# VectorE's attention and evictions in another order, projections one product earlier, the last operands h in the token buffers, stores behind the loads

## The reference

```python
xn = layernorm(x)
# attention: 32 heads of 16, 8 key/value heads, each token for itself
q, k, v = xn @ Wq + bq, xn @ Wk + bk, xn @ Wv + bv
k, v = repeat(k, 4), repeat(v, 4)
scores = einsum('bsdh,bseh->bsde', q, k) / 4        # 16 x 16 per token
s = einsum('bsde,bseh->bsdh', softmax(scores), v)
# gated feed-forward, 1792 hidden
nx = xn * rsqrt(mean(xn**2) + 1e-5) * ln_w
y = (silu(nx @ gate_w.T) * (nx @ up_w.T)) @ down_w.T
out = x + s * silu(y)
```

## Time and profile before

| | |
|---|---|
| three runs | 504.86 us median, 503.04 to 504.94 |
| profiled execution | 505.15 us, of which the span is 503.0 us |
| PE busy | 479.9 us (95%), 2148 matmuls |
| PEld busy | 394.8 us (78%) |
| DVE busy | 404.1 us (80%) |
| ACT busy | 225.1 us (45%) |
| POOL busy | 104.1 us (21%) |
| granted TensorE clock, mean | 0.996 |
| transfers | 105.12 MB, 209 GB/s |

### The profile page before, as it was taken

One profiled execution on the slowest core, in us unless ns is written; L12 is line 12 of the kernel. 1 busy time (PEld: TensorE's weight loads), 2 busy tenths in 40 slices (PEclk: granted clock), 3 DMA queues, 4 the chain that ended last, 5 costly groups with the idle time before them and its releaser, 6 DMA issues.

```text
span 503.0 us, 6150 instructions
## 1 busy us (share of the span) xinstructions
PE 479.9 (95%) x2148; PEld 394.8 (78%) x2148; DVE 404.1 (80%) x552; ACT 225.1 (45%) x373; POOL 104.1 (21%) x85
## 2 busy tenths in 40 slices
PE   7989999999999999989799989999999999999995
PEld 6778888777778888768788777887878788888873
DVE  6889788889889797849995968878886886876784
ACT  4573555576576564572113142432244243245222
POOL 3703222222222362335222101111111111112000
PEclk9999999999999999999899999999999999999999
DMA  8803799666666755772253557755555555414582
GB/s 256 319 1 151 289 331 362 247 249 250 249 247 246 264 219 213 251 270 95 85 170 123 182 215 248 294 189 208 208 210 210 188 188 189 188 43 153 185 289 85
DMA packets 27310, 105.12 MB, mean 209 GB/s; under 512 B 2832, under 2 KB 4112, under 8 KB 23952
## 3 DMA queue, kind: packets, MB, share of 16 engines
q1 hardware_dynamic: 27280, 104.74, 57.2%
HBM read 68.29 MB, written 36.44 MB: 208 GB/s over the span
## 4 chain that ended last, share of the span: by engine, by line
PE 57%; DVE 23%; ACT 8%; issue 7%; DMA 3%; SPq 1%; POOL 1%; DVEq 0%; ACTq 0%
PE gu_ps L430 12%; PE gu_ps L433 11%; PE gu_ps L432 11%; PE y_ps L561 4%; PE y_ps L560 4%; PE y_ps L562 4%; DVE prod L1063 3%; DVE scores L1066 2%; PE gu_ps L560 2%; PE gu_ps L562 2%; PE gu_ps L561 2%; DVE z_lo L980 2%; DVE prod L1081 2%; DMA xz<-x 2%; DVE attn L1084 1%
## 5 line engine op out<-in xcount | busy, mean ns | idle before, releaser
L430 PE MATMUL gu_ps<-z_hi,w_ops 128*128 128x512 f32 x364 | 143.8, 395 | 3.9 <-DVE h_kept L1044 1.5
L432 PE MATMUL gu_ps<-z_lo,w_ops 128*128 128x512 f32 x364 | 141.8, 390 | 0.0
L433 PE MATMUL gu_ps<-z_hi,w_ops 128*128 128x512 f32 x364 | 141.8, 390 | 0.0
L430 PEld LDWEIGHTS gu_ps<-z_hi,w_ops 128*128 128x128 f32 x364 | 68.3, 188 | 25.4 <-issue 6.5
L387 POOL TENSOR_TENSOR h_lo<-h,h_hi 128x512 fp32r<-128x512 f32 x28 | 38.3, 1370 | 204.3 <-ACT h_hi L792 204.3
L433 PEld LDWEIGHTS gu_ps<-z_hi,w_ops 128*128 128x128 f32 x364 | 68.3, 188 | 14.5
L432 PEld LDWEIGHTS gu_ps<-z_lo,w_ops 128*128 128x128 f32 x364 | 68.3, 188 | 13.4
L560 PE MATMUL y_ps<-wd_ops,h_hi 128*128 128x512 f32 x168 | 66.2, 394 | 2.4 <-POOL h_lo L387 2.3
L561 PE MATMUL y_ps<-wd_ops,h_hi 128*128 128x512 f32 x168 | 65.8, 391 | 0.0
L562 PE MATMUL y_ps<-wd_ops,h_lo 128*128 128x512 f32 x168 | 65.8, 391 | 0.0
L792 ACT ACTIVATE h_hi<-h 128x512 fp32r<-128x512 f32 x28 | 17.7, 632 | 98.3 <-DVE h L1032 98.3
(11 more groups left out here) (108 smaller groups left out, 747.6 us busy)
## 6 DMA issues: line engine op xcount, KB each, us to landing
w_kept<-w_ops SPq DMA_DIRECT2D x13, 1792.0 KB, 5.7
w_ops<-w_kept SPq DMA_DIRECT2D x13, 1792.0 KB, 7.4
wd_ops<-wd_kept SPq DMA_DIRECT2D x42, 512.0 KB, 4.0
raw<-gate_up SPq DMA_DIRECT2D x28, 256.0 KB, 3.3
wd_kept<-wd_ops SPq DMA_DIRECT2D x14, 512.0 KB, 7.2
xz<-x SPq DMA_DIRECT2D x16, 256.0 KB, 5.6
raw<-down SPq DMA_DIRECT2D x14, 256.0 KB, 7.3
xz<-x SPq DMA_DIRECT2D x2, 1024.0 KB, 5.8
```

The source lines that it names most:

```text
L430: pe.matmul(acc, w_h, z_hi[:, zi, c, :], start=start and c == 0, stop=False, skip_group_check=True)
L432: pe.matmul(acc, w_h, z_lo[:, zi, c, :], start=False, stop=False, skip_group_check=True)
L433: end = pe.matmul(acc, w_l, z_hi[:, zi, c, :], start=False, stop=c == 1, skip_group_check=True)
```

## The change

1. **Tokens' buffers for h.** From `FREE` = 43 on, `h_place(u)` puts both parts of h in `z_hi` and `z_lo`, which nobody reads after the last `m3`. Each of these 13 items has a place of its own, so ScalarE no longer waits for a buffer, but for the last `m3`. GpSimd makes all remainders, VectorE's `h_lo_part` is gone.
2. **Shares.** Each group has three portions: between `c12` and `times_up1` (second pass only), ahead of `c22`, behind it. The second pass has 104 steps in groups 14 to 27 instead of 114, the burst 29 instead of 35, so 33 steps instead of 17 are left behind the last group. `finish(1, j)` stands in groups 17, 18, 20 and 21 instead of 17 to 20.
3. **Takes earlier.** In the burst a take stands behind each portion and the `t_lo` behind the take, so product 8 is taken before any `t_lo`.
4. **Projections.** Product 3 runs before the first `gate1`; the second pass's eight each run one item earlier. On ScalarE `z_hi_tile` of tiles 5 to 7 and item 17's h stand earlier among `z_raw_tile`.
5. **Start.** The sum of the q bias goes from VectorE (one reduce) to GpSimd (two adds, between two `scale_tile`), and `lo_a(1)` goes ahead of take 4, take 6 ahead of `lo_s(1)`.
6. **Stores.** `store(2)` goes behind the last load.
7. ScalarE's last exponential comes behind all h; `t_hi(1, 3)` goes ahead of `y_out(1, ...)`.

```diff
+        FREE = ITEMS - NI + 1
+        def h_place(u):
+            if u < FREE:
+                return h_hi[:, u % 2, :], h_lo[:, u % 2, :]
+            m, c = divmod(u - FREE, 2)
+            return z_hi[:, m, c, :], z_lo[:, m, c, :]
...
-        PAIR_SHARES = (((0, 0), (1, 1), (2, 2), (2, 2), (2, 2), (2, 2), (2, 2), (2, 2), (0, 1), (1, 1), (1, 2),
-                        (2, 2), (1, 2), (1, 2)), ((5, 5),) + ((5, 3),) * (NI - 1))
-        SUM_SHARE = 2
-        BURST_SHARES = (5, 4, 4, 4, 3, 3, 3, 3)
+                       ((0, 3, 4), (0, 3, 2), (1, 5, 2), (1, 4, 2), (1, 4, 2), (1, 5, 2), (1, 4, 2), (1, 4, 2))
+                       + ((1, 5, 2),) * (NI - 8))
+        FINISH_IN = (3, 4, 6, 7)
+        BURST_SHARES = (2, 2, 2, 3, 4, 4, 5, 4, 3)
...
             def h_lo_part(u):
                 blk, n = item(u)
+                hi, lo = h_place(u)
                 pool.wait_ge(h_hi_done, u + 1)
-                wait(pool, d_done, J * (u - 1))
+                if u < FREE:
+                    wait(pool, d_done, J * (u - 1))
...
             scale_tile(J)
+            pool.wait_ge(bias_in, 48)
+            bias_quads = bq_raw.rearrange("p (n s r) -> p n s r", s=2, r=2)
+            pool.tensor_tensor(bias_quads[:, :, :, 0], bias_quads[:, :, :, 0], bias_quads[:, :, :, 1], ALU.add)\
+                .then_inc(bias_summed, 1)
+            pool.wait_ge(bias_summed, 1)
+            pool.tensor_tensor(bias[:, 0:DG], bias_quads[:, :, 0, 0], bias_quads[:, :, 1, 0], ALU.add)\
+                .then_inc(bias_summed, 1)
             scale_tile(J + 1)
...
             second_tile(J + 3)
+            qkv_product(3)
             gate1(0)
...
             for u in range(NI + 2, 2 * NI - 1):
                 down_product(u)
-                if u >= NI + 3 and u - NI - 3 < JJ:
-                    qkv_product(JJ + u - NI - 3)
+                if u - NI - 2 < JJ:
+                    qkv_product(JJ + u - NI - 2)
...
-                wait(act, d_done, J * (u - 1))
+                if u < FREE:
+                    wait(act, d_done, J * (u - 1))
+                else:
+                    act.wait_ge(m3_done, GROUPS)
...
             for u in range(ITEMS - NI, ITEMS):
                 load_wd(u)
-                if u == ITEMS - 4:
-                    store(2)
+            store(2)
             store(3)
```

More of the change, by code:

```diff
@@ L418, in _ @@
                     rms_of(0, JJ, 3, JJ)
-            for u in range(NI, LO_LAST):
+            for u in range(NI, ITEMS):
                 h_lo_part(u)
@@ L558, in down_tile @@
                 acc = gu_ps[:, j, :] if u >= 2 * NI and blk else y_ps[:, j, :]
[L559 to L563, removed]
+                hi, lo = (part[:, j * P:(j + 1) * P] for part in h_place(u))
+                pe.matmul(acc, hi, wd_ops[:, u % 3, 0, :], start=n == 0, stop=False)
+                pe.matmul(acc, hi, wd_ops[:, u % 3, 1, :], start=False, stop=False)
+                pe.matmul(acc, lo, wd_ops[:, u % 3, 0, :], start=False, stop=n == NI - 1).then_inc(d_done, 1)
             def down_product(u):
@@ L613, in _ @@
             second_tile(J + 3)
+            qkv_product(3)
             gate1(0)
             up1(0)
-            for index in range(3, JJ - 1):
+            for index in range(4, JJ - 1):
                 qkv_product(index)
@@ L871, in _ @@
             h_hi_part(NI + 2)
+            z_hi_tile(1, 5)
             z_raw_tile(1, 4)
-            for j in range(5, JJ):
-                z_hi_tile(1, j)
-                z_raw_tile(1, j)
+            z_hi_tile(1, 6)
+            z_raw_tile(1, 5)
             h_hi_part(NI + 3)
+            z_raw_tile(1, 6)
+            z_hi_tile(1, 7)
+            z_raw_tile(1, 7)
             for u in range(NI + 4, 2 * NI):
@@ L890, in _ @@
                 if g == NI + 1:
+                    t_hi(1, 3)
                     for j in range(J):
@@ L1166, in _ @@
             qkv_take(5)
+            qkv_take(6)
             lo_s(1)
[L1168 removed]
             t_lo(0, 3)
@@ L1172, in _ @@
                     c12(g - 1)
+                attention(shares[g][0])
                 if g + 1 < NI:
@@ L1196, in _ @@
                     lo_s(g + 1)
-                attention(shares[g][1])
+                attention(shares[g][2])
                 times_up0(g)
@@ L1205, in _ @@
                 t_add(1, n)
-            for n in range(3):
-                t_lo(1, n)
-                attention(SUM_SHARE)
-            for index in range(JJ, 2 * JJ):
-                qkv_take(index)
-                attention(BURST_SHARES[index - JJ])
+            for n, steps in enumerate(BURST_SHARES):
+                attention(steps)
+                if n < JJ:
+                    qkv_take(JJ + n)
+                if n < 3:
+                    t_lo(1, n)
             for j in range(J):
                 finish(0, j)
-            attention(shares[NI][0])
+            attention(shares[NI][1])
             times_up0(NI)
-            attention(shares[NI][1])
+            attention(shares[NI][2])
             times_up1(NI)
+            t_lo(1, 3)
             for g in range(NI + 1, GROUPS):
@@ L1221, in _ @@
                     c12(g - 1)
+                    attention(shares[g][0])
                     times_up1(g - 1)
-                else:
-                    t_lo(1, 3)
-                if 3 <= g - NI < 3 + J:
-                    finish(1, g - NI - 3)
-                attention(shares[g][0])
+                if g - NI in FINISH_IN:
+                    finish(1, FINISH_IN.index(g - NI))
+                attention(shares[g][1])
                 c22(g)
-                attention(shares[g][1])
+                attention(shares[g][2])
                 times_up0(g)
@@ L1232, in _ @@
             times_up1(LAST)
-            for u in range(LO_LAST, LO_LAST + 3):
-                h_lo_part(u)
-                attention(2)
+            attention(6)
             assert taken[0] >= values_end(3 * J - 1)
-            for u in range(LO_LAST + 3, ITEMS):
-                h_lo_part(u)
-                if u - LO_LAST - 3 < J:
-                    finish(2, u - LO_LAST - 3)
-                else:
-                    attention(3)
+            for j in range(J):
+                finish(2, j)
+                attention(4)
             attention(STEPS)
```

63 lines of the change are left out of this document (23 added, 40 removed).

## The result

The changed kernel takes 501.36 us (median of seven runs, 499.45 to 502.16) against 504.86 for the kernel before (seven runs, 503.04 to 505.81): ratio 0.9929, 95% interval 0.9909 to 0.9948. Forecast were 500.5 and a range of 493 to 506. The profiled execution, the slowest of the seven, took 502.16 us, span 500.4.

What follows compares the result with a forecast made beforehand. TensorE, busy 95% of the 503.0 us span, was taken as the bound. From 505.15: start +1.2, middle -8.8, groups -1.8, end +4.8 give 500.55, stated as 500.5; range 493.0 to 506.

Steps and rivals of the forecast that it cites:

- Start, +1.2 forecast: Up to m1(1): take 4 behind lo_a(1) comes at 42.3, product 6 waits 2.6 us; +1.2 us.
- the bound of +3.2: Start's upper bound: take 0 is 0.9 late and the clock falls as it did at 244 us.
- 0.5 later: Start: take 0 between 0.5 earlier and 0.8 later with GpSimd's bias adds; 0.5 later taken.
- Middle, -8.8 forecast: Where the second pass begins: waits for h_lo, take 8 and times_up(14) go, no clock fall; -8.8 us.
- The 0.4 that I charged: Middle: t_hi(1, 3) and four y_out fall ahead of take_u2(15) with no stall to cover them; 0.4 us lost.
- Rival B: Middle: GpSimd remainders keep takes late, second stall and clock fall stay (4.4 us); 504.9, no change; chance 0.15.
- Groups, -1.8 forecast: Groups 15 to 27: three waits for a seed and small gaps come to 2.2 us, 0.4 left; -1.8 us.
- End, +4.8 forecast: After group 27: 33 steps and GpSimd's remainders delay VectorE's last chain from 495.05 to 499.8; +4.8 us.
- GpSimd's share was 7.8 forecast: End: of 13 remainders costing 15 us, the part falling on VectorE moves its last chain from 492.0 by 7.8.
- Rivals A and C: End: A, GpSimd hidden under reduces, 493.9, chance 0.22; C, strict turns cost VectorE 15 us, 507.7, chance 0.08.
- TensorE's own gain here was put at 1.9 us: End: item 53's load no longer behind stores, no h waiting for a buffer; 1.9 us gained on TensorE.

Runs made afterwards that it cites:

- The middle with its single wait of 2.59 us: Changed kernel with only TensorE's and ScalarE's order in the middle put back, each projection one item later: 505.44 us, ratio 1.0012.
- the kernel with the thin remainders: Changed kernel with GpSimd's last 13 remainders taking one column instead of 512: 496.26 us, ratio 0.9822.

## Why the prediction was right, and where not

The direction and the mechanisms of the three large terms were right. That the total was forecast within 0.9 us is partly luck: along the span two errors of 3.3 and 1.15 us stand against 2.4 us that other stretches gave beyond the forecast, and the profiled execution is 1.7 us over 500.5.

**Start, +1.2 forecast, +4.45 measured: the mis-sized term.** The mechanism was the forecast one, take 4 behind `lo_a(1)`, and undoing it alone gave 3.7 us back. TensorE came to product 6 at 40.0 (forecast 40.2). Two sizes were off. Take 4 came at 43.0, not 42.3: of GpSimd's two operations of 2.2 us, which lie beside this stretch in both kernels, more now falls on VectorE, 2.32 instead of 1.79 us in the second `t_lo` and 2.01 instead of 1.51 in `lo_a`. And the clock was down behind the stall, 2.9 us here and 1.5 to 2.65 in other profiles of the same stall, which stood only in the bound; even the bound of +3.2 was too low. I had read from the earlier trace rows that TensorE stood twice ahead of the fall and took the second time for a condition. The middle with its single wait of 2.59 us shows that it is none.

The bias sum did what its working said and cost next to nothing: the add of 256 elements ran from 17.39 to 19.17 and take 0 came at 24.91, against 24.78 before, where 0.5 later was forecast.

**Middle, -8.8 forecast, -9.9 measured** (-8.2 and the 1.7 of `times_up1(14)`). Each named wait went. The two experiments show that neither half does it alone: with late takes the kernel is slower than before, with late projections the same. The 0.4 that I charged for `y_out` ahead of `take_u2(15)` was not paid, and the clock and the restarts gave some 0.7 more than taken. Rival B, takes held by GpSimd, fell: the four `t_add` took 5.98 us where the earlier trace rows has 6.92, and take 8 came before it was wanted.

**Groups, -1.8 forecast, -2.6 measured**: all small waits for a `seed` went, not all but 0.4. This is read from the waits alone; the shares of the groups were not put back, nor was the bias sum, nor the new places for h.

**End, +4.8 forecast, +4.5 measured.** Step by step: TensorE's last chain would have allowed the multiply at 485.7. VectorE without GpSimd is through at 482.9 + 0.4 = 483.3; the forecast, 492.0 in the times of before, is 483.8 when shifted by item 41's 8.2. GpSimd's share was 7.8 forecast (its own working, 15 - 5.8 - 1.1, gives 8.1), 8.1 measured. Rivals A and C, none of it and all of it, both fell. One term that the sum did not use was off: TensorE's own gain here was put at 1.9 us, and the kernel with the thin remainders, where TensorE sets the end, shows 40.38 - 39.23 = 1.15, since the load of item 55 is waited for 1.43.

**Behind VectorE's end, 0 forecast, +1.15 measured.** No step of the prediction covered it, and nothing in the diff points to it but that VectorE has 27 instructions fewer. It is a transfer of q14 on the last store, shown by the kernel in which only the number of VectorE's instructions differs.

## What to carry to other kernels

Moving an operation with two SBUF inputs from VectorE to GpSimd is worth what the trace says of the two side by side: here each cost VectorE 0.62 us in longer operations and would have cost it 0.56 to make. When a take or another releaser is moved, ask how long the engine behind it will stand, and carry the clock's fall behind it as a term with a chance of its own: here it cost from nothing to 2.9 us, and a single stall sufficed. Before two gains measured apart are added, cut both traces into stretches and see that each gain lies where its edit is. Parts of one reordering on several engines can be worse than nothing when one of them is missing, so test them by halves before crediting either.

## What the runs showed of the hardware

- TensorE's clock was down to 0.50 behind stalls of 2.59 us (at 230 us, 3 us long), 2.62 (at 241.7 in the kernel before), 3.53 (at 43.7), 3.97 (at 47.4, with product 3 put back) and 6.35 us (at 243, 5 us of work at 0.50); it was not behind one of 1.59 us at 42 us, one of 2.32 at 226 in the kernel before, nor, in the profiled run, one of 3.58 at 480 us. So these rows give no length above which a stall always brings it down.
- The same stall, 3.52 or 3.53 us ahead of product 6 in six profiles, cost 1.5 to 2.9 us of clock.
- Queue q14, named "instruction", has 13 transfers of about 8.5 KB (0.11 MB in all) while the program runs. One of them moved from 490.0 to 482.8 us when VectorE's program alone got 12 instructions longer; that it carries VectorE's code is read from that. A last store that met it took 3.2 instead of 2.0 us to land, in the profiles of eight versions with 712 instructions on VectorE; in a ninth it took 2.5. With 724, 725 and 739 it took 2.0.
- A GpSimd remainder of 1.3 us by itself took 21.71 / 13 = 1.67 us on average beside VectorE's attention, so both engines pay.
